# Attention of an MoE transformer layer: two pairs of heads per group, and values in one rotation of five PSUM banks

## The reference

```python
qg = split_heads(tokens @ Wqg, 16); kv = split_heads(tokens @ Wkv, 16)
queries, gates = qg[..., :16], qg[..., 16:]        # 64 gate columns per head
keys, values = kv[..., :16], kv[..., 16:]
queries, keys, values = l2norm(queries), l2norm(keys), l2norm(values)
attn = square(relu(einsum('bhid,bhjd->bhij', queries, keys)))
aggr = einsum('bhij,bhjd->bhid', attn, values)
out = tanh_norm(aggr) * tanh(silu(gates))
x = x + out @ Wout
# experts: sigmoid gate over 16 experts in 4 groups, best 2 groups, best 4 experts
inter = silu(x @ w_gate[e]) * (x @ w_up[e])        # 64 hidden columns per expert
x = x + sum_e combine[e] * (inter @ w_down[e]) + shared expert
```

## Time and profile before

| | |
|---|---|
| median of three runs | 685.98 us |
| profiled execution, its time | 687.0 us |
| its span | 685.3 us |
| PE busy | 646.5 us (94%) |
| DVE, ACT, POOL busy | 446.9, 427.7, 420.2 us |
| granted TensorE clock, mean | 0.998 |
| one step in the middle of the run | 38.87 us |

### The profile page before, as it was taken

One profiled execution on the slowest core, in us unless ns is written; L12 is line 12 of the kernel. 1 busy time (PEld: TensorE's weight loads), 2 busy tenths in 40 slices (PEclk: granted clock), 3 DMA queues, 4 the chain that ended last, 5 costly groups with the idle time before them and its releaser, 6 DMA issues.

```text
span 685.3 us, 15157 instructions
## 1 busy us (share of the span) xinstructions
PE 646.5 (94%) x5048; PEld 501.7 (73%) x5048; DVE 446.9 (65%) x1701; ACT 427.7 (62%) x986; POOL 420.2 (61%) x424
## 2 busy tenths in 40 slices
PE   2788998999999999999999999999999999999877
PEld 2555566777777778777778777878778787767777
DVE  5473647676766757576676767576675766555585
ACT  3578675666677675666776675666867566544312
POOL 3157855766757576776758585776768585686300
PEclk9999999999999999999999999999999999999999
DMA  9989949496784949497694949597694939503000
GB/s 253 142 136 150 118 102 114 103 139 108 131 135 102 107 132 122 88 154 117 121 134 109 112 131 112 98 148 124 115 131 101 121 102 124 101 5 76 9 1 16
DMA packets 75517, 76.14 MB, mean 111 GB/s; under 512 B 9296, under 2 KB 73392, under 8 KB 73648
## 3 DMA queue, kind: packets, MB, share of 16 engines
q1 hardware_dynamic: 75440, 75.17, 69.2%
HBM read 56.05 MB, written 19.10 MB: 110 GB/s over the span
## 4 chain that ended last, share of the span: by engine, by line
PE 84%; DVE 5%; ACT 5%; issue 3%; POOL 2%; DMA 1%; SPq 0%; DVEq 0%; ACTq 0%; POOLq 0%
PE ps_a L572 18%; PE ps_f L421 13%; PE ps_f L422 10%; PE ps_f L423 10%; PE ps_f L488 9%; PE ps_f L512 9%; PE ps_s L540 7%; PE ps_f L463 3%; PE ps_f L484 3%; POOL p L389 2%; PE ps_f L468 1%; PE ps_f L497 1%; DMA big<-in_L_attn_Wkv 1%; ACT r L678 1%; ACT sq L638 1%
## 5 line engine op out<-in xcount | busy, mean ns | idle before, releaser
L389 POOL TENSOR_TENSOR p<-r 128x512 f32<-128x512 f32 x256 | 260.9, 1040 | 177.5 <-ACT r L678 108.9
L572 PE MATMUL ps_a<-p,v 128*64 128x256 f32 x1024 | 145.5, 394 | 9.4 <-DVE big L994 4.7
L678 ACT ACTIVATE r<-ps_s 128x512 f32<-128x512 f32 x256 | 140.7, 613 | 13.5 <-PE ps_s L540 10.6
L994 DVE TENSOR_TENSOR big<-ps_a,big 128x256 f32<-128x256 f32 x128 | 54.1, 423 | 77.8 <-ACT big L687 77.2
L572 PEld LDWEIGHTS ps_a<-p,v 128*64 128x64 f32 x1024 | 64.4, 136 | 50.1 <-DVE big L994 7.7
L670 ACT ACTIVATE it<-ps_f 128x256 f32<-128x256 f32 x144 | 56.2, 390 | 49.4 <-PE ps_f L423 41.8
L408 POOL TENSOR_TENSOR it<-it,cb 128x512 f32<-128x512 f32 x56 | 71.2, 1282 | 18.9 <-DMA cb<-c_rows 18.8
L644 ACT ACTIVATE big<-ps_f 128x512 f32<-128x512 f32 x64 | 38.2, 598 | 66.2 <-PE ps_f L423 66.2
L949 DVE TENSOR_TENSOR it<-ps_f,it 128x256 f32<-128x256 f32 x144 | 60.6, 421 | 27.7 <-ACT it L670 26.5
L512 PE MATMUL ps_f<-wdown,it 128*128 128x128 f32 x576 | 70.4, 277 | 0.8 <-DVE it L966 0.8
L512 PEld LDWEIGHTS ps_f<-wdown,it 128*128 128x128 f32 x576 | 67.6, 192 | 2.4 <-DVE it L949 1.0
(11 more groups left out here) (159 smaller groups left out, 1430.1 us busy)
## 6 DMA issues: line engine op xcount, KB each, us to landing
qk_rows<-qk_parts SPq DMA_DIRECT2D x16, 1024.0 KB, 4.8
qkt<-qk_rows SPq DMA_DIRECT2D x64, 256.0 KB, 9.9
qkt<-qk_rows SPq DMA_DIRECT2D x128, 128.0 KB, 9.0
cb<-c_rows SPq DMA_DIRECT2D x28, 512.0 KB, 6.0
x_in<-in_L_attn_tokens SPq DMA_DIRECT2D x16, 128.0 KB, 6.3
x_res<-in_L_attn_tokens SPq DMA_DIRECT2D x16, 128.0 KB, 8.7
out<-o_sb SPq DMA_DIRECT2D x16, 128.0 KB, 8.6
big<-in_L_attn_Wqg SPq DMA_DIRECT2D x1, 640.0 KB, 4.5
```

Source lines behind the costliest of these rows:

```text
L389: pool.tensor_tensor(p[h % 4][:], r[h % 2][:], r[h % 2][:], ALU.mult).then_inc(probs_done, 1)
L572: last = pe.matmul(ps_a[64 * e:64 * e + 64, 0:N], v[s % 3][:, t, h * DV:(h + 1) * DV], p[h % 4][:, t * N:(t + 1) * N], start=(t == 0), sto ...
L678: act.activation(r[h % 2][:], ps_s[h % 2][:], ACT.Relu).then_inc(relu_done, 1)
```

## The change

PE's value matmuls become jobs of a new kind `av` with places in FILL: two of them at the end of slots 1, 3, 5 and 7. The bank ps_a joins the rotation, which now has five banks, and `wait_for_bank` looks five places back. In front of the first `av` of a slot stand the scores of the pair two ahead, behind the second the scores of the pair three ahead. ACT in an even slot does ReLU of pair k, the squares of pairs k-2 and k-1, and ReLU of pair k+1, then the evacuations. DVE gates two pairs in even slots. Semaphores `values_done` and `aw_done` become the `av` entries of `done` and `read`.

```diff
     FILL = [
         [("F", "lg", 0), ("P", "v", 3), ("D", "y2", 0), ("N", "ones", 0)],
-        [("N", "nT", 0), ("D", "y2", 1), ("P", "g", 0)],
+        [("N", "nT", 0), ("D", "y2", 1), ("P", "g", 0), ("A", "av", 0), ("A", "av", 1)],
         [("F", "gu", 0), ("F", "gu", 1), ("P", "g", 1), ("F", "gu", 2)],
-        [("F", "gu", 3), ("F", "cD", 0), ("P", "g", 2), ("O", "rT", 0), ("F", "gu", 4)],
+        [("F", "gu", 3), ("F", "cD", 0), ("P", "g", 2), ("O", "rT", 0), ("F", "gu", 4), ("A", "av", 2), ("A", "av", 3)],
         [("O", "rB", 0), ("O", "rB", 1), ("F", "gu", 5), ("O", "rB", 2), ("L", "xT", 0), ("O", "rB", 3), ("P", "g", 3)],
-        [("O", "y", 0), ("O", "y", 1), ("L", "qk", 0)],
+        [("O", "y", 0), ("O", "y", 1), ("L", "qk", 0), ("A", "av", 4), ("A", "av", 5)],
         [("F", "gu", 6), ("L", "qk", 1), ("L", "v", 0), ("F", "gu", 7)],
-        [("L", "v", 1), ("F", "gu", 8), ("O", "x2T", 0), ("L", "v", 2), SKIP, SKIP],
+        [("L", "v", 1), SKIP, ("F", "gu", 8), SKIP, ("O", "x2T", 0), SKIP, ("L", "v", 2), ("A", "av", 6), ("A", "av", 7)],
     ]
...
-            bank.update({job[1:]: ps_f[n % 4] for n, job in enumerate(order(s)) if job != SKIP})
+            bank.update({job[1:]: ps_f[n % 5] for n, job in enumerate(order(s)) if job != SKIP})
...
-                            wait(pool, values_done, 8 * s + (h - 4) // 2 + 1)
+                            wait(pool, done["av"], 8 * s + (h - 4) // 2 + 1)
...
                         if stage in on:
+                            if kind == "av" and j % 2 == 0:
+                                scores_ahead(s, q, j + 2)
                             wait_for_bank(n, s, at)
                             filler(stage, kind, j, s, q, on, at)
+                            if kind == "av" and j % 2 == 1:
+                                scores_ahead(s, q, j + 2)
                         n += 1
-
-                    if k < SLOTS - 1:
-                        if "A" in on:
-                            scores(s, q, k + 1)
-                    elif "A" in stages(at + 1):
-                        scores(s + 1, 1 - q, 0)
-                    if "A" in on:
-                        wait(pe, aw_done, 8 * s + k)
...
+                for k in range(SLOTS):
+                    if k % 2 == 0:
+                        relu(k)
+                        if ("A" in on and k > 0) or ("O" in on and k == 0):
+                            squared_heads(k)
+                        relu(k + 1)
...
-                    if ("A" in on and k > 0) or (O and k == 0):
-                        pair, ab = (k - 1, s) if k > 0 else (NP - 1, b)
-                        dve.wait_ge(a2_done, 8 * ab + pair + 1)
...
+                    if k % 2 == 0 and (("A" in on and k > 0) or (O and k == 0)):
+                        for i in range(2):
+                            pair, ab = (k - 2 + i, s) if k > 0 else (NP - 2 + i, b)
+                            ps = (bank if k > 0 else bank_before)[("av", pair)]
+                            dve.wait_ge(a2_done, 8 * ab + pair + 1)
```

More of the change, by code:

```diff
@@ L73, in order @@
         return [job for slot in fill(s) for job in slot]
-    assert all(len(plan) == SLOTS and sum(len(slot) for slot in plan) % 4 == 0 for plan in (FILL, *ENDS.values()))
+    assert all(len(plan) == SLOTS and sum(len(slot) for slot in plan) % 5 == 0 for plan in (FILL, *ENDS.values()))
     OFFSET = {"L": 2, "P": 1, "N": 1, "A": 0, "O": -1, "F": -2, "D": -3}
     JOBS = {"xT": 1, "qk": 2, "v": 4, "g": 4, "ones": 1, "nT": 1, "rT": 1, "rB": 4, "y": 2,
-            "x2T": 1, "lg": 1, "gu": FC, "cD": 1, "cT": 1, "cB": 4, "y2": 2}
+            "x2T": 1, "lg": 1, "gu": FC, "av": NP, "cD": 1, "cT": 1, "cB": 4, "y2": 2}
     BY_DMA = B - 2
@@ L474, in filler @@
                         last = pe.transpose(ps[0:2 * H, tok[t]], src[:, t, :, :].rearrange("p a h -> p (a h)"), ident[:])
+                elif kind == "av":
+                    last = values(b, j, ps)
                 elif kind == "cD":
@@ L544, in scores, with scores_ahead, values @@
                             last.then_inc(scores_done, 1)
+            def scores_ahead(s, q, k):
+                if k < NP:
+                    scores(s, q, k)
+                elif "A" in stages(s + 1):
+                    scores(s + 1, 1 - q, k - NP)
+            def values(b, k, ps):
+                if k in (0, 4):
+                    pe.wait_ge(v_normed, 4 * b + (2 if k == 0 else 4))
+                for t in range(T):
+                    for e in range(2):
+                        h = 2 * k + e
+                        if t == 0:
+                            pe.wait_ge(probs_done, 16 * b + h + 1)
+                        last = pe.matmul(ps[64 * e:64 * e + 64, 0:N],
+                                         v[b % 3][:, t, h * DV:(h + 1) * DV], p[h % 4][:, t * N:(t + 1) * N],
+                                         start=(t == 0), stop=(t == T - 1))
+                return last
             def step(s, q, on, at):
@@ L632, in evacuate @@
                     if j == 0:
-                        wait(act, values_done, 8 * (b - 2))
+                        wait(act, done["av"], 8 * (b - 2))
                     act.wait_ge(done[kind], count)
@@ L672, in step, with relu @@
             def step(s, q, on, at):
-                for k in range(SLOTS):
+                def relu(pair):
                     if "A" in on:
-                        for h in (2 * k, 2 * k + 1):
+                        for h in (2 * pair, 2 * pair + 1):
                             wait(act, probs_done, 16 * s + h - 1)
@@ L690, in step @@
                     for stage, kind, j in fill(at)[k]:
-                        if stage in on:
+                        if stage in on and kind != "av":
                             evacuate(stage, kind, j, s, q)
@@ L954, in scale_heads @@
                         dve.wait_ge(done["rB"], 4 * b + j + 1)
[L955 removed]
+                        dve.wait_ge(read["av"], 8 * b + 8)
                         part = heads3[b % 3][:, 2 * j:2 * j + 2, :]
@@ L987, in gated_heads @@
                 def gated_heads(k):
[L989 to L994 removed]
+                    if k % 2 == 0 and (("A" in on and k > 0) or (O and k == 0)):
+                        for i in range(2):
+                            pair, ab = (k - 2 + i, s) if k > 0 else (NP - 2 + i, b)
+                            ps = (bank if k > 0 else bank_before)[("av", pair)]
+                            dve.wait_ge(a2_done, 8 * ab + pair + 1)
+                            dve.wait_ge(gate_ready, 4 * ab + pair // 2 + 1)
+                            part = heads3[ab % 3][:, pair, :]
+                            dve.tensor_tensor(part, ps[:, 0:N], part, ALU.mult).then_inc(read["av"], 1)
                 def head_norm_roots():
```

50 lines of the change are left out of this document (17 added, 33 removed).

## The result

The changed kernel takes **730.67 us** (median of four runs, 728.33 to 733.74). The kernel before, run beside it, takes 686.63 us (four runs). The ratio is 1.0632, 95% interval 1.0572 to 1.0691: slower by 6.3%. The profiled execution took 728.33 us, with a span of 726.6, against 687.0 and 685.3 before.

A forecast was written before the change was run, and what follows sets the result against it. PE, busy 94% of the span, was taken as the bound; four waits net of tile savings add 3.43 us a step, 41.2 over twelve steps plus 3.5 elsewhere: 687.0 to 731.7, hence 731 us; range 697 to 748.

The forecast's parts named there:

- The sum: All steps: 38.87 to 42.30 us each, +3.43, over twelve steps 41.2 us, plus about 3.5 for other batches.
- Wait 1: Ones to nT, slot 7 to 1: nT waits for ACT's copy of n2row, no longer hidden; +0.46 us a step.
- The 3.5 for batches 0, 1, 14 and 15: First and last two batches: all have the first wait, the last two also the second and third; about 3.5 us.
- The gain: PE around attention: fewer tile-shape changes, a group from first scores to next job takes 2.78 us and saves 0.31.
- the rival of 669 us: Only the tile changes count, every input in time: 1.05 us a step back, 17 us faster; chance 0.09.
- Wait 2: Slot 1 to 3: cD waits for DVE's comb_rows, the next job for the bank of gu 1; +0.60 us a step.
- The ladder: After a mark: POOL's squares hold ACT's odd ReLU to 3.78 us, first Silu near 4.3, DVE's gate-up product at 4.74.
- The further 0.18 for the bank of gu 1: Behind cD: the next job waits another 0.18 us for the bank whose product DVE takes after comb_rows.
- Wait 3: Output rows, slot 3 to 5: y 0 waits for DVE's scaled heads, delayed by the late ReLU; +0.57 us a step.
- Wait 4: Slot 5 to 7: x2T waits for its rows and the bank of gu 7, behind packed ACT; +1.80 us a step.
- the late run to x2T is absorbed: Slots 6 and 7: ACT finds gaps, the x2T interval falls to -0.3, a step costs +1.3: 706 us; chance 0.20.

The follow-up runs named there:

- e13: Kernel before with each slot's scores moved ahead of its last job, adding one tile-shape change per slot: 709.24 us, ratio 1.0314.
- e7: e6 with slot 4 rewritten on PE and DVE (rB 0 to 3, xT, gu 5, g 3): 699.16 us, ratio 1.0169.
- e2: Changed kernel with job y2 0 moved between the ones sums and nT on all engines: 723.38 us, ratio 1.0493.
- e1: Changed kernel with ACT's ReLU of the odd pair moved back to the odd slot, behind the evacuations: 723.77 us, ratio 1.0508.
- e3: Changed kernel with job qk 0 moved ahead of y 0 and y 1 in slot 5: 720.39 us, ratio 1.0459.
- e5: Changed kernel with DVE's second norm and product of gu 7 ahead of the sums of v 0: 722.73 us, ratio 1.0504.
- e8: Rotation of five banks alone: values as jobs, one pair per slot, every engine's order as in the kernel before: 703.71 us, ratio 1.0234.
- e6: Changed kernel with the edits of e1, e2, e3 and e5 together: 702.64 us, ratio 1.0215.
- e12: Changed kernel with three r buffers instead of two; did not fit into on-chip memory, so no time.
- e11: Kernel before with only g 3 moved ahead of rB 2 in slot 4: 683.34 us, ratio 0.9920.

## Why the prediction was right, point by point

**The sum.** In the profiled execution the span grew by 41.3. The eleven steps of batches 3 to 13 give 11 x 3.20 = 35.2, the rest 6.1: first marks +0.5, batches 0 and 1 +1.8, batch 2 +1.4, batch 14 +0.3, tail +2.1. The prediction had 11 x 3.43 = 37.7 and 3.43 + 3.5 = 6.9 for the rest. Wait 1 was 0.05 too low, the other three intervals 0.19, 0.04 and 0.05 too high. The 3.5 for batches 0, 1, 14 and 15 isn't worked out: by its own terms it would be 4 x 0.46 + 2 x (0.60 + 0.57) = 4.2. The 731 against 730.67 is luck to that degree: on the profiled execution it is 731.7 against 728.33, and part of the difference between the two executions ahead of the steady steps may be the granted clock (last section).

**The gain.** A group takes 2.75 instead of 2.78, so it gives back 0.34 where the sum had 0.31. e13 shows from the other side that the 0.09 and 0.10 are time on the path. By these, a kernel with every input in time would be faster, as the rival of 669 us says. It never came about: even e7, with five repairs, has 39.15 a step.

**Wait 1** was +0.46 and is +0.51; e2 removes it and so shows its cause.

**Wait 2** was +0.60 and is +0.41. The ladder is the prediction's chain from ACT over POOL back to ACT and on to DVE. Its times were right to 0.15: ACT's last ReLU at 3.69 (predicted 3.78), the Silu at 4.18 (4.3), DVE's product at 4.59 (4.74), cD at 7.10 (7.18). The further 0.18 for the bank of gu 1 did not appear. As a cause the ladder is the smaller part. The prediction took the Silu's delay for POOL's hold on ACT. By e1, 1.28 of its 1.65 come from PE, which reaches gu 0 behind the whole group, and would be there without ACT's ladder. The prediction has no term for this, and the two paths end only 0.37 apart; that it took the later one is right, and e1 gives back 0.36.

**Wait 3** was +0.57 and is +0.53; y 0 started 6.75 after the mark, predicted 6.74. This near hit is luck, because the path was another. The prediction led it from the late ReLU over the Silu and the product of gu 5 to the scaled heads. e1 takes the ReLU away, and G3 to G5 stays at 11.19. ACT's Silu of gu 5 in e1, where G3 is at 330.08:

```profile
334.31 0.38 ACT L682 ACTIVATE it<-ps_f 128x256 f32<-128x256 f32 x1 [1.42 <-PE ps_f L424]
```

It starts 4.23 after the mark, as in the changed kernel, after ACT has waited 1.42 for PE. What holds the scaled heads is DVE's order. DVE in the kernel before (G3 at 313.52) and in the changed one (G3 at 330.87):

```profile
315.50 1.29 DVE L957 TENSOR_TENSOR big<-ps_f,big 128x512 f32<-128x512 f32 x2 [0.96 <-PE ps_f L484]
```

```profile
333.16 0.98 DVE L1019 TENSOR_TENSOR big<-ps_f,big 128x256 f32<-128x256 f32 x2 [0.99 <-ACT big L703]
334.15 1.29 DVE L980 TENSOR_TENSOR big<-ps_f,big 128x512 f32<-128x512 f32 x2
...
336.79 0.68 DVE L980 TENSOR_TENSOR big<-ps_f,big 128x512 f32<-128x512 f32 x1
```

The two gated pairs now come first and need ACT's square of the second pair, whose values PE makes at the end of the group. The first scaled heads start 3.28 after the mark instead of 1.98, and from the gated pairs to the last scaled heads DVE has no gap. This is read from the rows; no run moved the gated pairs alone. e3 puts a job of PE into the wait and fills 0.58 of it.

**Wait 4** was +1.80 and is +1.75, x2T 9.12 after the mark, predicted 9.23. The size was right, the reason only in part. I wrote that ACT is packed. It is, but e1 shows that with its ReLUs out of the way only 0.22 comes back, since PE hands over its jobs later too: gu 6 starts 3.23 after the mark (303.23) instead of 1.44 (325.62 in the kernel before). The sum was right because it carried the spacing of the earlier trace rows along, and that spacing contains DVE's sums of v 0. DVE in the changed kernel, ahead of x2T at 309.12:

```profile
308.13 0.61 DVE L781 SCALAR_TENSOR_TENSOR xn<-x,mv,ps_d 128x128 f32<-128x128 f32 x2
308.65 0.75 DVE L972 TENSOR_TENSOR it<-ps_f,it 128x256 f32<-128x256 f32 x2
```

Ahead of these rows DVE idles 0.29 for ACT's square and then takes 0.69 for the sums; e5 moves both out of the way and gains 0.97. The rows of x2T are there at 308.74, and x2T then waits for the product of gu 7 (0.42 from 308.65, so 309.07), which frees its bank five places back. With four banks it was the bank of v 0, so about 0.3 of this wait belongs to the rotation. The rival *the late run to x2T is absorbed* thus had a true premise: most of ACT's delay is no loss. It failed because what hides the delay, PE's late hand-over, makes DVE's chain late as well: the product of gu 7 ends 9.07 after the mark instead of 7.05, while PE, with one interruption less on the way, is ready for x2T at about 7.9 instead of 7.43.

**What wasn't foreseen.** The second scores at G5 end 0.49 late for ps_s, which the prediction put at nothing, with the remark that it would come if ACT were later. The job gu 8 ahead of x2T starts some 0.3 late. Both lie in the 10.19 and made up for a shorter gap ahead of x2T (1.2). And I treated the rotation as neutral, beyond the bank of x2T. e8 prices it at 1.56 a step in the old order. Its two waits aren't in the steady steps of the changed kernel, so that price is not part of the 3.20. The rotation comes back as a wait of the values at G7 as soon as the repairs make PE early (e6, e7).

**Left open.** What a third buffer r is worth stays an estimate, as e12 gave no result. Whether grouping with perfect tables gets under 38.45 a step is open too, and so is what the rotation costs with other places of the jobs.

## What to carry to other kernels

Merging changes of tile shape saves a measurable price (here some 0.3 us a group), but it also puts dependent jobs next to each other, hands the jobs behind the group to the follower engines later (here 1.3 us), and makes their work come in lumps. For every job, work out when its input is ready from the chain of in-order engines, and compare that with when the first engine gets there. If private buffers join a rotation, each member waits for the reader of the job so many places back, so the rotation needs its price even where no instruction moves. A number that comes out right doesn't show the path: the stations of the ladder over ACT were forecast to 0.15 us, and e1 shows that most of what they were to explain came from the order on PE and DVE. Repairs need not add up, as a wait that is removed can uncover the next (0.97 alone, 0.10 behind the others); and a plain reordering in the one slot where PE waited (e11) was worth more than all of it.

## What the runs showed of the hardware

The granted TensorE clock in the first 60 us differs between executions, and the profiled executions of the two kernels differ in it. The windows of the changed kernel, and behind them one of the kernel before (columns: window, its length, busy time of PE, its weight loads, DVE, ACT and POOL with counts, granted clock, DMA share, GB/s):

```profile
0.00:20.00 20.00, 7.37 (x24) 5.47 (x24) 10.17 (x32) 9.01 (x16) 6.21 (x17) 0.91 0.98 253
20.00:40.00 20.00, 10.89 (x62) 8.48 (x62) 13.43 (x37) 13.88 (x26) 2.75 (x3) 0.91 1.10 119
40.00:60.00 20.00, 16.94 (x98) 11.25 (x99) 7.75 (x31) 13.13 (x27) 14.51 (x15) 0.74 0.98 138
```

```profile
40.00:60.00 20.00, 16.07 (x115) 9.94 (x111) 11.01 (x35) 15.99 (x34) 15.85 (x17) 1.00 0.96 140
```

A share of each of the changed kernel's three windows ran at the lower of the two levels (1.2 GHz, against 2.4); in the first of them PE was busy for 7.4 of 20 us. It is no mark of the change: e11 has 0.58 in its window from 20 to 40 and is the fastest kernel here, e13 has 1.00 in all three, and other executions of the kernel before had means from 0.975 to 0.998 with times between 683.75 and 693.26. How much of that spread of some 1% is the clock was not separated. From 100 to 120 us both kernels' windows have 0.91; from 120 us to the end of the steady steps both have 1.00 in every window, so the steady steps compare at one clock.
